# Attention block with a token-choosing feed-forward: both halves of a key tile's values behind two steps of score and maximum pairs

## The reference

```
q = x @ Wq
kv = x @ Wkv
q, kv = split(q), split(kv)          # 8 * 16 heads of 1024 x 16
q, kv = rotary(q), rotary(kv)
att = einsum('bmd,bnd->bmn', q * SCALE, kv)
attn = softmax(att, axis=-1)
out = einsum('bij,bjd->bid', attn, kv)
x = x + out @ Wout + bout
```

## Time and profile before

| what | value |
|---|---|
| median of 3 runs | 2364.81 us |
| lowest and highest of the 3 | 2360.68 and 2385.1 us |
| the profiled execution | 2362.94 us |
| its span | 2361.0 us |
| PE busy | 2068.3 us (88%) |
| DVE busy | 1991.6 us (84%) |
| ACT busy | 1494.4 us (63%) |
| POOL busy | 703.7 us (30%) |

### The profile page before, as it was taken

One profiled execution on the slowest core, in us unless ns is written; L12 is line 12 of the kernel. 1 busy time (PEld: TensorE's weight loads), 2 busy tenths in 40 slices (PEclk: granted clock), 3 DMA queues, 4 the chain that ended last, 5 costly groups with the idle time before them and its releaser, 6 DMA issues. The chain is left out here.

```text
span 2361.0 us, 53852 instructions
## 1 busy us (share of the span) xinstructions
PE 2068.3 (88%) x16812; PEld 1064.6 (45%) x16812; DVE 1991.6 (84%) x3212; ACT 1494.4 (63%) x2850; POOL 703.7 (30%) x880
## 2 busy tenths in 40 slices
PE   6777699999999999999999999999675149988998
PEld 3334233333333333333333333335343138887897
DVE  7888799999999999999999999946446688887874
ACT  3444288888888888888888888872223024333333
POOL 7788101011111111011111111015333046665664
PEclk9999599999999999999999999999778569999999
DMA  3667534444444444433334444433443033333332
GB/s 96 216 220 202 182 71 82 82 75 77 76 76 81 79 80 81 82 78 76 75 75 81 80 79 81 82 118 99 142 162 112 9 101 80 79 75 76 91 64 30
DMA packets 152669, 224.66 MB, mean 95 GB/s; under 512 B 34855, under 2 KB 105098, under 8 KB 152586
## 3 DMA queue, kind: packets, MB, share of 16 engines
q1 hardware_dynamic: 140262, 206.61, 36.7%
q0 software_dynamic: 12288, 17.05, 4.5%
q10 hardware_dynamic: 36, 0.02, 0.0%
HBM read 129.45 MB, written 93.06 MB: 94 GB/s over the span
## 5 line engine op out<-in xcount | busy, mean ns | idle before, releaser
L761 DVE TENSOR_REDUCE a_mx<-a_sm 128x2 f32<-128x1024 f32 x1024 | 1234.1, 1222 | 55.1 <-PE a_sm L709 41.4
L836 ACT ACTIVATE a_prob<-a_st 128x512 f32<-128x512 f32 x2048 | 1112.7, 597 | 166.6 <-PE a_st L672 135.8
L672 PE MATMUL a_st<-a_q,a_k 50*128 50x512 f32 x2048 | 750.3, 447 | 6.3 <-DMA a_q<-a_mrow 6.3
L709 PE MATMUL a_sm<-a_k,a_q 48*128 48x512 f32 x2048 | 747.4, 454 | 9.3 <-DVE a_mx L761 7.6
L696 PE MATMUL a_pv<-a_prob,a_v 128*32 128x256 f32 x8192 | 655.9, 392 | 23.1 <-ACT a_oraw L843 22.5
L672 PEld LDWEIGHTS a_st<-a_q,a_k 50*128 50x128 f32 x2048 | 311.3, 185 | 411.5 <-ACT a_prob L836 391.5
L811 POOL TENSOR_TENSOR a_v<-a_v_raw,a_zero 128x256 f32<-128x256 f32 x64 | 39.6, 620 | 1049.3 <-DMA a_v_raw<-values 1032.9
L696 PEld LDWEIGHTS a_pv<-a_prob,a_v 128*32 128x32 f32 x8192 | 161.8, 108 | 394.6 <-issue 190.4
L709 PEld LDWEIGHTS a_sm<-a_k,a_q 48*128 48x128 f32 x2048 | 304.5, 188 | 21.4 <-DVE a_mx L761 19.2
L1769 ACT ACTIVATE e_hT<-e_ps_h,e_b1b 128x512 f32<-128x512 f32 x128 | 88.1, 689 | 276.6 <-PE e_ps_h L1803 267.4
L1803 PE MATMUL e_ps_o<-e_w_high,e_hT_high 128*128 128x256 f32 x512 | 152.7, 298 | 25.8 <-DVE e_biased L1674 25.8
(11 more groups left out here) (148 smaller groups left out, 2418.9 us busy)
## 6 DMA issues: line engine op xcount, KB each, us to landing
qkv_parts<-p_parts SPq DMA_DIRECT2D x64, 512.0 KB
a_q<-qkv_parts SPq DMA_DIRECT2D x128, 128.0 KB, 3.6
a_k<-qkv_parts SPq DMA_DIRECT2D x128, 128.0 KB, 4.4
attended<-a_oraw SPq DMA_DIRECT2D x64, 256.0 KB, 4.0
e_w<-in_fc_dram SPq DMA_DIRECT2D x16, 1024.0 KB, 5.3
token_table<-f_tab SPq DMA_DIRECT2D x8, 1056.0 KB, 7.3
p_x<-in_x_dram SPq DMA_DIRECT2D x16, 512.0 KB, 8.0
values<-p_values SPq DMA_DIRECT2D x8, 1024.0 KB, 20.1
```

The costliest lines, as they stand in the source:

```text
L672: nc.tensor.matmul(st[:, slot % RING], kb[rows, q.buf, jt * P:(jt + 1) * P], qb[rows, q.buf, ic * CHUNK:(ic + 1) * CHUNK], start=True, sto ...
L709: mm = nc.tensor.matmul(sm[:, slot, h], qb[rows, q.buf, qt * P:(qt + 1) * P], kb[rows, q.buf, kc * CHUNK:(kc + 1) * CHUNK], start=True, st ...
L761: nc.vector.tensor_reduce(mx[:, qt, kc, :], sm[:, slot], AX.X, ALU.max, negate=True).then_inc(max_done, 1)
L836: nc.scalar.activation(prob[:, jt % 2, h, ic * CHUNK:(ic + 1) * CHUNK], st[:, slot % RING], ACT.Exp, scale=DH ** -0.5).then_inc(drained, 1)
```

## The change

In `body` of PE's part of `attend`, the values are issued in odd steps alone, both parts of the key tile one after the other. Part 1 stays where it was, at the end of an odd step; part 0 moves from the end of the even step to just ahead of it. In steps 0 and 1 of a pair the same is done with the last key tile of the pair before. What is computed, the tiles, the number of buffers and all instructions of the other engines stay as they were.

```
@@ -726,10 +726,12 @@
                 scores(q, 2 * g + 1)
                 if ahead.exists():
                     maxima(ahead, v, g % 2, 0)
-                if g >= 2:
-                    values(q, g // 2 - 1, g % 2)
-                elif not q.first():
-                    values(q.plus(-1), TILES - 1, g % 2)
+                if g % 2 == 1:
+                    for part in range(2):
+                        if g >= 2:
+                            values(q, g // 2 - 1, part)
+                        elif not q.first():
+                            values(q.plus(-1), TILES - 1, part)
```

## The result

The changed kernel takes 2457.23 us (median of 4 runs, 2451.99 to 2461.67) against 2362.74 us (4 runs, 2359.42 to 2385.1): a ratio of 1.0379, 95% interval 1.032 to 1.0438. It is slower by about 94 us, on the side and at the size forecast (2458, range 2395 to 2500). Its profiled execution took 2451.99 us with a span of 2450.2.

A forecast was written before the change was run, and what follows sets the result against it. PE's order was taken as the bound, 2.45 us per two steps. Grouped, these take 1.26 + 0.43 + 1.00 = 2.69: 511 x 0.24 less 63 x 0.44 gives +95 on 2362.94, so 2458 us, range 2395 to 2500.

The forecast's parts named there:

- PE as the bound before: In attend, PE's order sets the pace at 1.23 us a step; DVE has 0.10 and ACT 0.25 to spare.
- PE's own work: Two steps (even, then odd) on PE alone, with values grouped: 2.10 us against 2.45 if nothing else were late.
- values to the next A0: From the grouped values' start to the next even step's first score pair: 0.57 + 0.43 = 1.00 us.
- B0 to A1: Even step's second score pair to odd step's first, no values between: 0.22 us, from half-clock rows.
- The ring's wait: Odd step's second score pair waits for the exponential of the even step's first, starting 1.26 us after that pair, not 0.78.
- The late weight load: The waiting second score pair of an odd step loads weights only at its start: 0.43 us to values instead of 0.32.
- rival 1: The ring waits, but weights load ahead: odd step's second pair to values stays 0.32, +38 us, 2401; chance 0.13.
- The others: DVE and ACT keep up in each two steps; the next even step's successor has its maxima covered by 0.04 us.
- The start of a head pair: Values' wait for the copy of a_pv in step 2 goes: 0.44 us freed, 63 times; exponential delay taken as 0.
- rival 2: The wait at the odd step's second score pair costs 0.19 more: two steps take 2.88, +192 us, 2555; chance 0.10.
- rival 3: DVE's two buffers of maxima, not the ring, hold up the odd step's first pair: -33 us, 2330; chance 0.07.
- rival 4: Only PE's changes between pairs and values count; DVE's 2.26 sets two steps' pace: -125 us, 2238; chance 0.04.

The follow-up runs named there:

- one_after5: Changed kernel's order with head 0's maxima products left out, as one_after3, but five banks in the ring of scores instead of three: 2323.09 us, ratio 0.9813 to before.
- one_after3: Changed kernel's order with head 0's maxima products left out (DVE reads head 1's twice), ring of three banks: 2463.84 us, ratio 1.04 to before.
- mix_half: Full computation: against the kernel before, key tiles 0, 2, 4 and 6 have both parts of values together, the others unchanged: 2407.35 us, ratio 1.0162.
- one_before3: Kernel before, in its own order, with head 0's maxima products left out and a ring of three banks: 3276.04 us, ratio 1.383.

## Why the prediction was right

*PE as the bound before.* This was read from start times, and it carried the rest: all terms are distances between starts on PE.

*PE's own work.* Forecast 2.10 for a double step that waits for nothing; 2.12 in one_after5. The term values to the next A0, forecast 1.00, is 1.00 (907.91 to 908.91). B0 to A1 was the one taken from rows at half clock: 0.22 forecast, 0.23 measured. The Trainium skill, "TensorEngine Tiling (Array Packing)", section Key Properties, says that a change of tiling mode drains the array. The traces agree that such a change has a price, since pairs of a kind follow at 0.23 and a pair and values at 0.32; that a drain is the reason, they don't show. And the price saved wins nothing while another wait is last.

*The ring's wait.* 1.26 forecast, 1.26 measured (0.61 + 0.60 + 0.05), and shown by one_after3 and one_after5, which differ only in the number of banks.

*The late weight load.* 0.43 forecast, 0.44 measured (907.47 to 907.91), with B1 0.50 long and its load starting with it. The Trainium skill, "TensorE: Matmul & The Clock Gate", has in its table of specifications that PE's queue pulls weight loads ahead of matmuls in flight; here it doesn't do so for a pair held by a semaphore. The prediction read rows 4 too widely, though, when it said that loads run ahead for the pairs that don't wait: that holds for second pairs. A0, behind values, waits for no exponential either, and its load starts with it (900.43 and 900.44 before, 908.90 and 908.91 after); first pairs last 0.50 as well. The term itself stands: in one_after5, the same order with B1 free to start, the values follow B1 by 0.32 (904.54 to 904.86), as rival 1 had it, and where B1 waits they follow by 0.44. This decided between 2458 and rival 1's 2401.

*The others.* That the odd step's maxima would be covered held by a hair, as worked out, and where it didn't (mix_half) the ring was still last.

*The start of a head pair.* The wait of 0.44 went, as forecast. But ACT's copy does push back the exponential behind it, to 0.70 after the step's first score (956.11 - 955.41) instead of 0.60, and with it B1 (956.76, +1.35):

```profile
955.41 0.50 PE L672 MATMUL a_st<-a_q,a_k 50*128 50x512 f32 x1
956.76 0.50 PE L672 MATMUL a_st<-a_q,a_k 50*128 50x512 f32 x1 [0.34 <-ACT a_prob L838]
958.20 0.50 PE L672 MATMUL a_st<-a_q,a_k 50*128 50x512 f32 x1
```

```profile
955.63 0.59 ACT L845 COPY a_oraw<-a_pv 128x512 f32<-128x512 f32 x1 [0.23 <-PE a_pv L696]
956.11 1.09 ACT L838 ACTIVATE a_prob<-a_st 128x512 f32<-128x512 f32 x2
```

The bounds for this were 0 and 0.12 and I took 0. The copy started 0.22 after the step's first score, not 0.13, though ACT had been idle for 0.23 by then: it starts later behind the values' end than the row at the end of the stage let me expect. It costs 63 x 0.09 = 6 us. Two smaller readings were off without weight in the sum: in slice 27 DVE stands at 4 tenths and ACT at 7, and 896.19 is 0.25 behind the copy's end, not 0.24.

*Total.* Forecast +95 on the profiled execution, measured +89. The head pairs gave +93, since the 6 us just named were made up by a step of before that was on average a little longer than 1.225: (20.36 - 0.44 - 0.26) / 16 = 1.229, where 0.26 is the turn of the maxima on PE (903.48 to 903.74 in one_after5's timeline), so that a double step lost 0.23 and not 0.24. What lies ahead of the first copy, which the sum left out, gave -4, with a higher clock in that stretch (0.90 and 0.79). By the two levels of the changed kernel's times, 9 us apart, this is the luck of one execution and not of the order. The medians lie +94 apart.

*The rivals.* Rival 1 fell by the 0.44; rival 2 (register work behind the wait) by the same number; rival 3 by one_after3 and by B1's start; rival 4 by the ring, though one_after5 shows what it rests on.

## What to carry to other kernels

Before work on one engine is bunched, count what the bunching puts next to each other: with a ring of three banks, four fills in a row wait for the first one's reader, however idle that reader is on average. The check needs three durations (start to reader's start, the reader's own, the hand-back) against the distance between fill n and fill n+3, and a waiting product pays for its late weight load as well. And look for such a wait in the start times: idle time by engine showed 0.23 of 0.46 in one kernel and nothing in another.

## What the runs showed of the hardware that was not expected

With the order of before and half of the maxima products left out, the granted clock stayed at 0.50 for the whole attention stage, in both rings, while PE was busy throughout by the profile. The whole stage with five banks:

```profile
303.00:2480.00 2177.00, 2176.97 (x11039) 706.11 (x11036) 1229.46 (x1111) 1136.44 (x2123) 140.62 (x246) 0.50 0.18 47
```

The kernel before, with all products, went to full clock inside its first head pair (0.79 on average from 276 to 303 us, then 1.00), and so did the changed order with the same products left out:

```profile
276.00:303.00 27.00, 26.05 (x182) 11.84 (x182) 20.79 (x19) 18.57 (x37) 0.46 (x2) 0.73 0.48 148
303.00:1600.00 1297.00, 1159.29 (x10497) 528.68 (x10501) 1134.57 (x1069) 1024.44 (x2018) 133.70 (x236) 1.00 0.40 73
```

These are the two levels of the clock, 1.2 and 2.4 GHz. Less work for PE made the kernel take 38% longer here, since a step that is 1.23 us at full clock took 2.16 (901.33 to 903.49 in one_before3):

```profile
901.33 0.79 PE L672 MATMUL a_st<-a_q,a_k 50*128 50x512 f32 x1
903.49 0.79 PE L672 MATMUL a_st<-a_q,a_k 50*128 50x512 f32 x1
```

Why the one order comes out of the half clock and the other doesn't stays open: no run varied it apart from the order. The length of the ring made no difference.
